# An attention loop rebuilt: row-tiled scores, q's norm folded into the mask step, and a new order of work on five engines

## The reference

```python
h = shift_token(x);  q, k, v = split(h @ wqkv)          # 8 heads of 64
q = l2norm(q) * qs;  k = l2norm(k) * ksc
q, k = rotary_xpos(q, k)                                # q*cos*scale + rotate_half(q)*sin*scale
# blocks of 128 queries look at their own block and the one before: 256 keys
sim = (8 * q) @ k.T;  sim = where(mask, -max, sim)
x = x + softmax(sim) @ v @ wo
```

## Time and profile before

| what | value |
|---|---|
| median of 3 runs | 2107.81 us (2107.7 to 2108.52) |
| span of the profiled execution | 2108.3 us |
| PE, DVE, ACT, POOL busy in it | 87%, 68%, 46%, 38% |
| granted TensorE clock, mean | 0.936 of full speed |
| first to last scores of the attention loop, layer 0 | about 532 to 1033 us |
| the same, layer 1 | about 1310 to 1812 us |

### The profile page before, as it was taken

One profiled execution on the slowest core, in us unless ns is written; L12 is line 12 of the kernel. 1 busy time (PEld: TensorE's weight loads), 2 busy tenths in 40 slices (PEclk: granted clock), 3 DMA queues, 4 the chain that ended last, 5 costly groups with the idle time before them and its releaser, 6 DMA issues.

```text
span 2108.3 us, 38778 instructions
## 1 busy us (share of the span) xinstructions
PE 1823.9 (87%) x10590; PEld 1396.6 (66%) x10590; DVE 1438.1 (68%) x4211; ACT 977.4 (46%) x2550; POOL 799.5 (38%) x963
## 2 busy tenths in 40 slices
PE   3868669993999999999799995999999999799990
PEld 1222448772777777777588874777777777578870
DVE  3664436675888888888755554888888888655554
ACT  1110105452677677777522212777767777422220
POOL 4000024565333333333345553333433333444545
PEclk8879779996999999999899997999999999899995
DMA  3100001112000000000010002000000000100005
GB/s 115 50 0 0 0 0 56 61 64 84 11 4 4 4 5 4 4 5 4 13 49 10 10 10 58 4 4 5 4 4 5 4 4 5 54 7 9 9 10 164
DMA packets 58388, 48.23 MB, mean 23 GB/s; under 512 B 9957, under 2 KB 56313, under 8 KB 58361
## 3 DMA queue, kind: packets, MB, share of 16 engines
q1 hardware_dynamic: 58360, 47.94, 7.2%
HBM read 29.05 MB, written 8.39 MB: 18 GB/s over the span
## 4 chain that ended last, share of the span: by engine, by line
PE 73%; DMA 6%; DVE 5%; SPq 5%; POOL 4%; ACT 3%; issue 3%; POOLq 1%; DVEq 0%; ACTq 0%; PEldq 0%; PEld 0%
PE bank L1157 11%; PE bank L1188 7%; PE bank L1163 5%; PE bank L1136 5%; PE bank L1179 5%; PE bank L1257 5%; PE bank L1137 4%; PE bank L1138 4%; PE bank L1258 4%; PE bank L1259 4%; SPq L438 4%; PE bank L1148 3%; PE bank L1022 3%; DMA x_in<-in_L_attn_hidden_states 2%; ACT pT L871 2%
## 5 line engine op out<-in xcount | busy, mean ns | idle before, releaser
L649 POOL TENSOR_TENSOR rnorm<-sumsq,neg_half 128x8 f32<-128x8 f32 x132 | 217.0, 1644 | 621.5 <-DVE sumsq L1567 621.5
L860 ACT ACTIVATE prob<-prob,neg_max 128x256 f32<-128x256 f32 x512 | 256.2, 503 | 161.9 <-DVE neg_max L1598 161.8
L1157 PE MATMUL bank<-kT,qT 128*128 128x256 f32 x1032 | 267.8, 383 | 1.7 <-DVE kT L1584 1.7
L936 ACT ACTIVATE gelu_sb<-bank,b_sb 114x512 f32<-114x512 f32 x96 | 66.2, 690 | 348.5 <-PE bank L1259 346.4
L1157 PEld LDWEIGHTS bank<-kT,qT 128*128 128x128 f32 x1032 | 197.3, 191 | 35.1 <-issue 2.5
L710 POOL TENSOR_TENSOR act_lo<-act_full,act_hi 114x512 fp32r<-114x512 f32 x96 | 128.2, 1336 | 204.4 <-PE bank L1274 152.9
L1136 PE MATMUL bank<-wqkv_hi,hT_hi 128*128 128x512 f32 x396 | 195.4, 493 | 2.0 <-DVE hT_lo L1543 2.0
L1188 PE MATMUL bank<-pT,v_sb 128*64 128x128 f32 x2048 | 168.3, 285 | 16.0 <-ACT pT L871 16.0
L1720 DVE SCALAR_TENSOR_TENSOR act_full<-bank,b_sb,gelu_sb 114x512 f32<-114x512 f32 x96 | 71.0, 740 | 152.3 <-PE bank L1259 152.3
L1257 PE MATMUL bank<-h_hi,w_hi 128*114 128x512 f32 (+1 forms) x384 | 156.2, 407 | 21.1 <-POOL h_lo L683 11.1
L1188 PEld LDWEIGHTS bank<-pT,v_sb 128*64 128x64 f32 x2048 | 106.5, 136 | 88.3 <-issue 57.1
(11 more groups left out here) (226 smaller groups left out, 4289.0 us busy)
## 6 DMA issues: line engine op xcount, KB each, us to landing
x_in<-in_L_attn_hidden_states SPq DMA_DIRECT2D x16, 512.0 KB, 3.5
hs_attn<-x_sb SPq DMA_DIRECT2D x24, 254.0 KB
raw<-in_L_ffn_wqkv SPq DMA_DIRECT2D x3, 1536.0 KB, 6.8
x_scratch<-x_in SPq DMA_DIRECT2D x8, 512.0 KB, 4.2
f_x<-x_scratch SPq DMA_DIRECT2D x8, 512.0 KB, 4.3
out<-f_y SPq DMA_DIRECT2D x8, 512.0 KB, 3.2
hs_ffn<-x_sb SPq DMA_DIRECT2D x64, 63.5 KB
raw<-in_L_ffn_w SPq DMA_DIRECT2D x2, 1364.0 KB
```

What stands on the lines that cost most here:

```text
L649: pool.tensor_tensor(rnorm[:, part], sumsq[:, part], neg_half[:, part], ALU.pow).then_inc(r_ready[which], 1)
L860: act.activation(prob[:, h], prob[:, h], ACT.Exp, bias=neg_max[:, h:h + 1], scale=-1.0, accum_out=psums[:, h:h + 1]).then_inc(exped, 1)
L1157: mm = pe.matmul(bank[:, 3 + j % 2, e * 2 * P:(e + 1) * 2 * P], qT[:, j, e], kT[:, j].rearrange("p a b -> p (a b)"), start=True, stop=True)
```

## The change

Only the attention loop changes. All that the diff below touches:

- Scores: `qT` holds a pair of heads in 128 rows, with no zeros. A head's score matmul takes 64 rows (`rows64`); the two heads of a pair write to different PSUM banks. They are issued in two groups of four heads.
- The scale of `hide` is now q's norm, `rnorm[:, h:h+1]`, instead of 1.0; q itself isn't normalised. `BIG` becomes 1e25.
- Scaling of `prob`: seven heads on DVE, head 3 on POOL, none on ACT. Reciprocals come two at a time (`inverses`), each followed by a wait on itself.
- `add_k` moves from DVE to POOL (`add_up`), q's copy out of PSUM wholly to ACT, the squares get a buffer of their own.
- The order on PE: block k - 1's last values and its output projection lie in block k. The last block of a layer no longer projects a block that isn't there.

PE's new order, and DVE's:

```diff
+                def scores(k, part):
+                    for j in (2 * part, 2 * part + 1):
+                        for e in range(2):
+                            rows64 = slice(e * DH, (e + 1) * DH)
+                            mm = pe.matmul(bank[:, 3 + e, (j % 2) * 2 * P:(j % 2 + 1) * 2 * P], qT[rows64, j],
+                                           kT[rows64, j].rearrange("p a b -> p (a b)"), start=True, stop=True)
+                    mm.then_inc(s_ready, 1)
...
+                def block(t, first, hT_next, final):       # PE
+                    pe.wait_ge(kT_ready, k + 1)
+                    pe.wait_ge(qT_ready, k + 1)
...
+                    scores(k, 0)
+                    if not first:
+                        values(k - 1, 2)
+                        values(k - 1, 3)
+                    if not final:
+                        project(f, 1, qk_raw[1])
+                    if not first:
+                        project_out(k - 1)
+                    pe.wait_ge(masked, HEADS * k + 4)
+                    scores(k, 1)
+                    if not final:
+                        project(f, 0, qk_raw[0])
+                    turn_probs(k, 0)
+                    if not first:
+                        pe.wait_ge(x_attn, 1 + k)
+                    turn_probs(k, 1)
+                    pe.wait_ge(v_ready, 1 + f)
+                    if not final:
+                        project(f, 2, v_raw)
+                    if hT_next:
+                        pe.wait_ge(masked, HEADS * k + HEADS)
+                        transposes(f + 1)
+                    values(k, 0)
+                    values(k, 1)
+                    if not final:
+                        turn_qk(f, 1)
+                        turn_qk(f, 0)
+                    turn_probs(k, 2)
+                    turn_probs(k, 3)
...
+                def sums(f, which):                         # DVE
                     dve.wait_ge(squares[which], f + 1)
+                    dve.tensor_reduce(sumsq[:, part], qk_sq[:, which].rearrange("p (h d) -> p h d", d=DH),
                                       AX_X, ALU.add).then_inc(ss_ready[which], 1)
                     dve.wait_ge(ss_ready[which], f + 1)
                     settle(dve)
                     dve.tensor_scalar(sumsq[:, part], sumsq[:, part], 1e-24, None, ALU.max).then_inc(ss_floor[which], 1)
...
+                def inverses(k, h):
+                    dve.wait_ge(exped, HEADS * k + h + 2)
+                    dve.reciprocal(pinv[:, h:h + 2], psums[:, h:h + 2]).then_inc(inverted, 1)
+                    dve.wait_ge(inverted, 4 * k + h // 2 + 1)
                     settle(dve)
...
+                def block(t, i, first, hT_next, final):     # DVE
+                    for h in range(4):
+                        hide(i, k, h)
+                    if not final:
                         sums(f, 1)
+                    inverses(k, 0)
+                    weigh(0)
+                    weigh(1)
+                    if not final:
                         cosines(f, t + 1, 1)
                         sines(t + 1, 1)
+                    inverses(k, 2)
+                    weigh(2)
+                    if not first:
+                        add_rows(t - 1)
+                    for h in range(4, 8):
+                        hide(i, k, h)
+                    if not final:
+                        normalise_k(f)
+                        cosines(f, t + 1, 0)
+                        sines(t + 1, 0)
+                        sums(f, 0)
+                    inverses(k, 4)
+                    weigh(4)
+                    weigh(5)
+                    if hT_next:
+                        lo(f + 1)
+                    inverses(k, 6)
+                    weigh(6)
+                    weigh(7)
+                    if not final:
                         k_out(f, 1 - i)
```

POOL's order in a block is `stage_h(t + 2)`, `root(f, 1)`, `weigh(k, 3)`, `add_up(f, 1)`, in every second block the copy of a mask, `add_up(f, 0)`, `root(f, 0)`. ACT's:

```diff
+                def block(t, i, first, final):              # ACT
+                    exponent(k, 0)
+                    if not first:
+                        values_out(k - 1)
+                    exponent(k, 1)
+                    if not final:
+                        square(f, 1)
+                    exponent(k, 2)
+                    exponent(k, 3)
+                    v_out(k, i)
+                    exponent(k, 4)
+                    exponent(k, 5)
+                    if not final:
+                        square(f, 0)
+                    probs_out(k, 0)
+                    exponent(k, 6)
+                    probs_out(k, 1)
+                    exponent(k, 7)
+                def block_end(t, hT_next, final):
+                    if hT_next:
+                        hi(f + 1)
+                    if not final:
+                        q_out(f)
+                    probs_out(k, 2)
+                    probs_out(k, 3)
```

More of the change, by code:

```diff
@@ L663, in _, with block_pair @@
-                with pool.Fori(0, NB // 2) as u:
+                root(k0, 1)
+                add_up(k0, 1)
+                add_up(k0, 0)
+                root(k0, 0)
+                pool.wait_ge(hT_ps, k0 + 1)
+                settle(pool)
+                stage_h(1)
+                def block_pair(u, ends):
                     for i in range(2):
                         t = u * 2 + i
-                        front(f0 + t + 1)
+                        k = k0 + t
+                        f = k + 1
+                        final = ends and i == 1
+                        if not ends:
+                            pool.wait_ge(hT_ps, k + 2)
+                            settle(pool)
+                            stage_h(t + 2)
+                        if not final:
+                            root(f, 1)
+                        weigh(k, 3)
+                        if not final:
+                            add_up(f, 1)
@@ L1601, in _ @@
-                lo(f0 + lay)
-                for which in range(2):
-                    sums(f0, which)
-                    floor_sums(f0, which)
-                    cosines(f0, 0, which)
-                    sines(0, which)
-                lo(f0 + lay + 1)
-                add_k(f0)
-                normalise(f0, 0)
-                normalise(f0, 1)
-                q_even_out(f0)
-                k_out(f0, 0)
-                dve.wait_ge(mask_set, lay * (NB // 2 + 1) + 1)
-                hide(0, lay * NB, 0)
@@ new lines, in _ @@
+                k0 = lay * NB
+                lo(k0)
+                sums(k0, 1)
+                cosines(k0, 0, 1)
+                sines(0, 1)
+                cosines(k0, 0, 0)
+                sines(0, 0)
+                sums(k0, 0)
+                lo(k0 + 1)
+                normalise_k(k0)
+                k_out(k0, 0)
+                def block(t, i, first, hT_next, final):
+                    k = k0 + t
+                    f = k + 1
+                    for h in range(4):
+                        hide(i, k, h)
+                    if not final:
@@ new lines, in block @@
+                    inverses(k, 6)
+                    weigh(6)
+                    weigh(7)
+                    if not final:
+                        k_out(f, 1 - i)
+                block(0, 0, True, True, False)
+                block(1, 1, False, True, False)
+                with dve.Fori(1, NB // 2 - 1) as u:
+                    for i in range(2):
+                        block(u * 2 + i, i, False, True, False)
+                block(NB - 2, 0, False, False, False)
+                block(NB - 1, 1, False, False, True)
@@ L1660, in _ @@
+                add_rows(NB - 1)
                 end_phase(dve, 5 + 4 * lay)
```

329 lines of the change are left out of this document (127 added, 202 removed).

## The result

| | before | after |
|---|---|---|
| median | 2107.76 us (2106.01 to 2108.52, 4 runs) | 2143.31 us (2140.82 to 2147.03, 4 runs) |
| profiled span | 2108.3 us | 2139.4 us |
| a block of the attention loop | 15.63 us | 16.32 us, median of the blocks of both layers |

The ratio is 1.018, 95% interval 1.0158 to 1.0203. The change costs 1.8%, 36 us. Forecast were 2140 us and 16.23 us a block.

A forecast was written before the change was run, and what follows sets the result against it. PE bound the kernel before; afterwards a loop through PE, ACT and DVE: 15.40 + 0.63 + 0.2 = 16.23 us a block, 0.60 more; 62 blocks +37, ends -5, +32 on 2108.3 gives 2140 us, range 2075 to 2200.

The forecast's parts named there:

- ring: Attention block: loop from first scores through PE, ACT, DVE and back to PE, 15.40 us before port waits.
- PE's start behind `kT`: End of the loop: PE starts the next block's scores 0.14 us after DVE has written kT.
- `weigh(2)` or `add_up(f, 1)` in the way: k's part of the block: DVE's scaling waits for POOL, or POOL's addition ends later; 0.2 us a block.
- Hide's new operand: q's norm as scale in `hide` on DVE: taken as nothing, bounded by 0.1 us for each of four hides.
- The port: `sums(f, 0)`: DVE's floor of q's sums held until POOL's addition ends, 0.63 us; at `weigh(2)` another 0.2.
- Values, round trips, PE's part: Loop's start on PE: scores 0.87, values 0.87, three half round trips 0.45, k's projection 1.67; together 3.86 us.
- The ends: First and last block of each layer: about 1.2 us less and 18 down to 16.5; 5 us in all.
- What would show it: Signs in the profile after: blocks 16.2 us apart, PE busy some 13.3, DVE idle 1.9 ahead of k's reduce, paired scores.
- ring without port waits: Rival: POOL's additions fall beside other work or waits are shorter; 15.40 us a block, 2089 us, chance 0.18.
- Unpaired scores: Rival: score records over 64 rows don't run in pairs; 0.87 us more a block, 2194 us, chance 0.12.
- Port held through two operations: Rival: POOL holds the port through `weigh(k, 3)` and `add_up(f, 1)`; 1.29 us more a block, 2220 us, chance 0.10.
- PE as the bound: Rival: the loop is shorter and PE's work sets the time; 13.5 us a block, 1971 us, chance 0.10.

The follow-up runs named there:

- e_k_short: The changed kernel without the two matmuls of the low part of the input in k's projection: 2116.15 us, ratio 1.0037 to the kernel before.
- f_v_short: The changed kernel without the two matmuls of the low part of the input in v's projection: 2145.75 us, ratio 1.0187 to the kernel before.
- g_hide_const: The changed kernel with the constant 1.0 in place of q's norm as the scale of `hide`: 2143.60 us, ratio 1.0176 to the kernel before.
- k_const_sq: The changed kernel with the constant 1.0 as scale of `hide` and ACT's square of q ahead of two exponents: 2134.31 us, ratio 1.0123.
- c_pe_waits: The changed kernel with only kT's wait left ahead of PE's scores, the other four ahead of the previous block's last transposes: 2124.44 us, ratio 1.009.
- d2_full_rows: The changed kernel with every score matmul taking all 128 rows of qT and kT: 2204.25 us, ratio 1.0464 to the kernel before.
- the three edits: The changed kernel with reciprocals and two scalings ahead of k's sums, q's floor later, and PE's waits moved: 2064.61 us, ratio 0.9791.
- a_inv_first: The changed kernel with the first pair's reciprocals and two scalings ahead of the sums of k's squares on DVE: 2100.03 us, ratio 0.9973.
- h_addq_dve: The changed kernel with the addition joining q's two halves done by DVE, no longer by POOL: 2160.95 us, ratio 1.0248.

## Why the prediction was right, point by point

The mechanism was the one forecast: a ring through PE, ACT and DVE. e_k_short and f_v_short show it. That the sum came out so close is in part luck. Hides and PE's start behind `kT` were 0.45 us a block too small, and pieces that were too large took back 0.42; and the span of 2139.4 us holds a first stage that was 8.5 us shorter for another reason. By the marks in both traces the change costs 36.8 us where 32 were forecast. The pieces, for the block from 786.10 to 802.41:

| piece | forecast | measured |
|---|---|---|
| PE and ACT, first score to reduction of k | 4.52 | 4.42 |
| `sums(f, 1)`, inverses, two scalings | 1.78 | 1.81 |
| rotation of k, inverses, scaling, `add_rows` | 2.13 | 2.15 |
| four hides, `normalise_k` | 1.96 | 2.23 |
| rotation and reduction of q, to the floor | 2.03 | 2.03 |
| floor, with the wait for POOL's addition | 0.72 | 0.66 |
| inverses, four scalings, `lo` | 2.06 | 2.00 |
| `kT`, and PE's start behind it | 0.83 | 1.01 |
| `weigh(2)` or `add_up(f, 1)` in the way | 0.20 | 0.00 |
| sum | 16.23 | 16.31 |

- **Hide's new operand.** Forecast at nothing, bounded by 0.1 each. It is 0.06 each (g_hide_const, k_const_sq): +0.24 us a block. The step failed in its size.
- **ACT beside the hides.** The forecast followed DVE alone between the hides and q's rotation. ACT's path is as long, and the prediction didn't see it. It cost nothing, but it hid the price of the operand.
- **PE's start behind `kT`.** I took 0.14 from the prologue, where PE has four waits; with five in the loop it is 0.33 to 0.44, and with kT's alone 0.05 (c_pe_waits). Mis-sized by 0.2 to 0.3.
- **The port.** 0.63 forecast for q's floor, 0.57 measured. The Trainium skill (SBUF — State Buffer, Who interferes with whom) has the port pair that DVE and POOL share as taken for a whole instruction by whoever issues first, and the 0.73 us floor that ends with POOL's addition agrees. The 0.2 at `weigh(2)` wasn't there. DVE got in 0.05 us ahead of POOL (793.84, 793.89), and the records of the two scalings overlap (0.37 and 0.58 long), where I had put POOL's behind DVE's. So POOL's addition ended at 795.71, 0.2 earlier than forecast, and `normalise_k` started at 796.09; with hides as fast as before it would have been 795.85, still behind it.
- **Values, round trips, PE's part.** 3.86 forecast, 3.79 measured (786.10 to the square's start at 789.89, which holds the 0.03 of ACT). The prediction says that the earlier trace rows agree with the skill on tiles of 64 rows; those rows show halves of the output columns only. For 64 rows it is d2_full_rows that shows it: 1.99 us against 1.14.
- **The ends.** I had given the first block 1.2 us less than the others. It takes 16.59, more than they do, since PE starts it at the lower of its two clocks (granted 0.50 from 524.36 to 526.44, 1.2 GHz): its score group spans 2.08 us, not 1.14. But the first block of the kernel before was long too, 16.81 and 18.23 us in the two layers, so there still was something to gain. The last block is shorter by 2.2, where I had said 1.5, and the stretch ahead of the loop is longer by 1.0. With 31 x 0.69 = 21.4 us a layer for the blocks and 19.1 and 17.7 measured, the ends are worth 6.0 us where 5 were forecast. What was too low is the block: 0.09 us, 62 times.
- **What would show it.** DVE's idle time was forecast at 1.9 and is 1.39; slower hides in front of it are 0.24 of the difference (four times 0.06) and PE's shorter part 0.10, the rest I can't place. PE was forecast busy for 13.3 us of a block and is for 14.75.

The rivals: *ring without port waits* is refuted by the 0.73 us floor. *Unpaired scores* by d2_full_rows, which stands where that rival was put (2204 against 2194), far from the changed kernel's 2143. *Port held through two operations* didn't come about, since DVE was first (793.84); what POOL would have held had it been first isn't shown. *PE as the bound* by f_v_short; its 13.5 us seems too low as well, since PE's records, whose ends are modelled, cover 14.41 us of a block even with the three edits. What decided between faster and slower lies in the ring: with a_inv_first alone, the same operations in another order, the change is a small gain.

## What to carry to other kernels

When a change takes load off the busiest engine, follow one iteration from engine to engine until it closes on itself, and add up its pieces: here the busiest engine lost work and the kernel lost time. Then ask of every operation in that ring whether it must be there; three edits that move work out of it, or waits off it, were worth 3.8%, and none takes arithmetic away. An experiment that removes the same work once inside and once outside the supposed ring settles the question in two runs.

## What the runs showed that I had not expected

- The records of score matmuls over 64 rows start in pairs, 14 to 19 ns apart, even if the program puts both matmuls of one half of the rows first, and the group takes the same 1.14 us. What makes up such a pair is open.
- A per-partition operand in place of a constant makes the mask-and-max operation on 256 elements 0.06 us longer (0.34 to 0.40 from start to start).
- Waits of PE that are long met still cost: the scores start 0.05 us after their input with one wait there, 0.13 with three, 0.33 to 0.44 with five.
- POOL's power over eight elements, 1.65 us, takes 2.08 where a DVE addition of two SBUF operands started just ahead of it (h_addq_dve: 772.10, 771.98). Beside DVE's scalings in the changed kernel it takes 1.65, and they aren't longer either (799.66; two scalings from 799.70 in 0.62).
